# Two-layer recurrent block on one core: retention products and the last gather moved in the slot order, B taken ahead of the gate, and half of the rank comparisons replaced by row sums

## The reference

```
xn = layernorm(x)
s  = retention(xn)                      # q k^T with decay GAMMA^(i-j), times v
g  = silu(w3 . gelu(h2 . gelu(h1 . (silu(w1 xn) * (w2 xn)))))    # ternary weights, 512 hidden
x  = x + s * g
xn = layernorm(x)
a, gate = split(xn @ W_in + b_in)
xc = silu(causal_conv4(a))
B, C = split(xc @ W_x + b_x)            # 16 states
h_t = A * h_(t-1) + xc_t (x) B_t        # a scan over the sequence for 128 x 16 states
s  = ((C_t . h_t) + D * xc_t) * silu(gate) @ W_out + b_out
# mixture of depths: the 512 best of 1024 tokens by the router's score get an update
w  = sigmoid(top-512 scores);  g = silu(xn + [token chosen] * w * ffn(xn))
x  = x + s * g
```

## Time and profile before

| | us |
|---|---|
| median of three runs | 546.86 |
| lowest, highest | 544.11, 549.14 |
| the profiled execution | 545.56 |
| its span (first to last instruction) | 543.8 |

### The profile page before, as it was taken

One profiled execution on the slowest core, in us unless ns is written; L12 is line 12 of the kernel. 1 busy time (PEld: TensorE's weight loads), 2 busy tenths in 40 slices (PEclk: granted clock), 3 DMA queues, 4 the chain that ended last, 5 costly groups with the idle time before them and its releaser, 6 DMA issues.

```text
span 543.8 us, 6040 instructions
## 1 busy us (share of the span) xinstructions
PE 443.4 (82%) x1777; PEld 259.0 (48%) x1791; DVE 407.9 (75%) x659; ACT 291.4 (54%) x475; POOL 404.7 (74%) x316
## 2 busy tenths in 40 slices
PE   0796978898889897989899888989798999485743
PEld 0575645644564455545565456445554464131211
DVE  2282144959788977989598959898789779958985
ACT  3664736774567545763676366745676447313300
POOL 1673543887599959985999769985999599855582
PEclk9997979899999999999999999999999999978865
DMA  8300006311513143221532162214321332215220
GB/s 316 136 20 4 1 0 175 85 51 40 155 60 86 50 125 108 77 77 47 152 96 78 37 176 77 79 39 118 115 79 58 96 99 78 78 44 165 85 74 19
DMA packets 25379, 46.97 MB, mean 86 GB/s; under 512 B 3072, under 2 KB 4096, under 8 KB 25088
## 3 DMA queue, kind: packets, MB, share of 16 engines
q1 hardware_dynamic: 24336, 45.13, 28.1%
q10 hardware_dynamic: 1008, 1.41, 0.8%
HBM read 42.33 MB, written 4.19 MB: 86 GB/s over the span
## 4 chain that ended last, share of the span: by engine, by line
POOL 35%; DVE 23%; issue 17%; PE 16%; ACT 5%; DMA 1%; SPq 0%; DVEq 0%; POOLq 0%; ACTq 0%
POOL hs L548 15%; DVE hs L1359 10%; PE bank0a L932 7%; DVE xbank L1336 7%; POOL hidAl L510 6%; POOL hidBl L510 5%; PE bank1a L1012 2%; POOL xnTl L492 2%; POOL g L526 2%; POOL g L522 2%; DMA Bt<-w_in 1%; POOL xr L530 1%; POOL q L499 1%; PE ybank L1071 1%; DVE st L1262 1%
## 5 line engine op out<-in xcount | busy, mean ns | idle before, releaser
L548 POOL TENSOR_TENSOR hs<-hs,Ct 128x512 f32<-128x512 f32 x127 | 184.6, 1459 | 32.6 <-DVE hs L1359 19.7
L510 POOL TENSOR_TENSOR hidAl<-plain,hidAh 128x512 fp32r<-128x512 f32 x48 | 64.6, 1346 | 37.7 <-ACT hidAh L643 31.3
L1359 DVE TENSOR_TENSOR_SCAN hs<-decay,carry,xbank 128x512 f32<-128x512 f32 x63 | 80.5, 1278 | 7.6
L510 POOL TENSOR_TENSOR hidBl<-plain,hidBh 128x512 fp32r<-128x512 f32 x48 | 66.1, 1378 | 26.6 <-ACT hidBh L643 18.7
L1359 DVE TENSOR_TENSOR_SCAN hs<-decay,xbank 128x512 f32<-128x512 f32 x64 | 78.0, 1219 | 5.6 <-DVE xbank L1336 0.5
L1336 DVE TENSOR_TENSOR xbank<-xs,bbank 128x512 f32<-128x512 f32 x104 | 71.4, 687 | 1.3
L642 ACT ACTIVATE plain<-bank0a,col 128x512 f32<-128x512 f32 x64 | 44.2, 690 | 45.2 <-PE bank0a L932 44.0
L932 PE MATMUL bank0a<-hidBh,hTh 128*128 128x512 f32 x128 | 57.7, 451 | 1.7 <-ACT q L675 1.7
L932 PE MATMUL bank0a<-hidAh,hTh 128*128 128x512 f32 x128 | 57.0, 445 | 1.7 <-ACT q L675 1.7
L932 PE MATMUL bank0a<-hidAl,hTh 128*128 128x512 f32 x128 | 51.6, 403 | 0.0
L932 PE MATMUL bank0a<-hidBl,hTh 128*128 128x512 f32 x128 | 50.7, 396 | 0.0
(11 more groups left out here) (184 smaller groups left out, 951.7 us busy)
## 6 DMA issues: line engine op xcount, KB each, us to landing
xs<-x_rows SPq DMA_DIRECT2D x128, 256.0 KB, 3.4
xt<-x_tok SPq DMA_DIRECT2D x8, 256.0 KB, 4.5
xr<-x_feat SPq DMA_DIRECT2D x8, 256.0 KB, 7.6
x_rows<-xc SPq DMA_DIRECT2D x8, 256.0 KB, 2.0
out<-xr SPq DMA_DIRECT2D x7, 256.0 KB, 2.2
fh<-h_w SPq DMA_DIRECT2D x1, 1024.0 KB, 10.0
hs<-h_w SPq DMA_DIRECT2D x1, 1024.0 KB, 11.9
lw<-l_w ACTq DMA_DIRECT2D x1, 640.0 KB, 5.4
```

The lines of the kernel that those rows point to most:

```text
L510: pool.tensor_tensor(low[:, m, :], plain[:, k % NPLAIN, :], high[:, m, :].bitcast(F32), ALU.subtract).then_inc(hidden_low, 1)
L548: pool.tensor_tensor(h, h, Ct[:, hs_(u)], ALU.mult).then_inc(p_ready, 1)
L1359: dve.tensor_tensor_scan(hs[:, i % NSTATES, :], decay[:, gr:gr + 1].broadcast_to([P, HALF]), xbank[:], 0.0 if u % 2 == 0 else carry[:, k:k ...
```

## The change

There are six edits.

1. `scores` goes from slot 2 to slot 4 of PE, and `outer` from the end of slot 4's list to slot 5, behind B's projection and ahead of the gate's. `mask_scores` goes from slot 2 to 4 and `memory` from 4 to 6 on DVE, and `scale_q` from 5 to 6 on POOL. The order of `bank0d` becomes z2 of tile 1, z2 of tile 3, scores, outer.
2. The projection of B goes ahead of that of the gate, on PE and on ACT (`take_B` directly behind the conv).
3. `stats_l0` goes from slot 7 to 5 on DVE and `rstd_l0` from 8 to 6 on POOL.
4. `gather_y` of the last quad goes from slot 8 to 9, behind `retention_out` and `retention_in`; `gate_y` from 9 to 11. The last unit keeps its slot.
5. Odd units no longer do `compare_other`. The even unit before compares in four instructions of 512 columns whose row sums (`counts`) tell for each token of the odd unit how many tokens of the even one beat it. In the rank of the odd unit four small matmuls with the identity bring these counts in place of four matmuls over comparisons. In the even unit's rank the comparison is turned round, so it is summed with a matrix of minus ones and compared with TOPK - HALF.
6. The same order in the run-in: `scores(0)` behind all of z2, the mask behind all four `z_product`.

```diff
@@ orders of the banks
-        L0_DVE += [("z2", _v, 1), ("scores", _v), ("z2", _v, 3), ("outer", _v)]
+        L0_DVE += [("z2", _v, 1), ("z2", _v, 3), ("scores", _v), ("outer", _v)]
-        L1_ACT += [(_k, _n) for _k in ("xnT", "conv", "gate", "B", "C", "score", "score_col")]
+        L1_ACT += [(_k, _n) for _k in ("xnT", "conv", "B", "gate", "C", "score", "score_col")]
@@ POOL slot
-                if w is not None and s == 8:
+                if w is not None and s == 6:
                     rstd_l0(w)
                 if u is not None:
                     weigh_states(u, k)
-                if v is not None and s == 5:
+                if v is not None and s == 6:
                     scale_q(v)
@@ ACT slot
                     if s == 5:
                         convolved(n)
+                        take_B(n)
                         take_gate(n)
...
-                    if s == 6:
-                        take_B(n)
-                    elif s == 7:
+                    if s == 7:
                         take_C(n)
@@ PE rank
-                    pe.wait_ge(beats_ready, r + 1)
-                    pe.matmul(bank1d[:], ones[:], beats[:, r % NBEATS, :], start=(pos == 0),
-                              stop=(pos == CH - 1)).then_inc(l1_dve_full if pos == CH - 1 else ranked, 1)
+                    full = l1_dve_full if pos == CH - 1 else ranked
+                    if u % 2 == 1 and pos >= CPH:
+                        j = pos - CPH
+                        pe.matmul(bank1d[:, ck(j)], counts[:, j:j + 1].broadcast_to([P, P]), ident[:], start=False,
+                                  stop=(pos == CH - 1)).then_inc(full, 1)
+                        return
+                    pe.wait_ge(beats_ready, beats_of(u) + pos + 1)
+                    pe.matmul(bank1d[:], ones[:] if pos < CPH else minus_ones[:], beats[:, r % NBEATS, :],
+                              start=(pos == 0), stop=(pos == CH - 1)).then_inc(full, 1)
@@ PE slot
-                        elif s == 2:
+                        elif s == 4:
                             scores(v)
-                        elif s == 4:
-                            outer(v)
...
                         elif s == 5:
-                            project("gate", n, W_IN[:, P:2 * P])
-                        elif s == 6:
                             project_x("B", n, W_B)
+                    if v is not None and s == 5:
+                        outer(v)
+                    if n is not None and s == 5:
+                        project("gate", n, W_IN[:, P:2 * P])
...
-                    if s == 8 and t is not None:
-                        gather_y(t, 3)
...
+                    if t is not None and s == (8 if t == UNITS - 1 else 9):
+                        gather_y(t, 3)
@@ DVE compare_other
-                other = u // 2 * 2 + 1 - u % 2
...
-                dve.tensor_tensor(beats[:, CPH:], row.broadcast_to([P, CPH, HALF]), s_i.broadcast_to([P, CPH, HALF]),
-                                  ALU.is_le if u % 2 else ALU.is_lt).then_inc(beats_ready, CPH)
+                for j, c in enumerate(chunks(u + 1)):
+                    dve.tensor_scalar(beats[:, CPH + j, :], srow[:, hs_(u)], scol[:, u // 2 % 2, c:c + 1], 0.0, ALU.is_ge,
+                                      ALU.add, accum_out=counts[:, j:j + 1]).then_inc(beats_ready, 1)
@@ DVE slot
-                    if s == 2:
+                    if s == 4:
                         mask_scores(v)
-                    elif s == 4:
+                    elif s == 6:
                         memory(v)
                 if t is not None:
-                    if compare_slots(t)[CPH] == s:
+                    if t % 2 == 0 and compare_slots(t)[CPH] == s:
                         compare_other(t)
...
-                    elif t < UNITS - 1 and s == 9:
+                    elif t < UNITS - 1 and s == 11:
                         gate_y(t)
...
-                    if s == 7:
+                    if s == 5:
                         stats_l0(w)
```

More of the change, by code:

```diff
@@ L118, in compare_slots, with beats_of @@
     return (-5, -4, -3, -2) + ((0, 0, 0, 0) if u == UNITS - 1 else (10, 10, 10, 10))
+def beats_of(u):
+    return u // 2 * (CH + CPH) + u % 2 * CH
 def rank_slots(u):
@@ L207, in program @@
         ones = sb("ones", [P, P], BF16)
+        minus_ones = sb("minus_ones", [P, P], BF16)
+        counts = sb("counts", [P, CPH])
         half_neg = sb("half_neg", [P, CH])
@@ L470, in _ @@
             pool.memset(ones[:], 1.0).then_inc(consts_set, 1)
+            pool.memset(minus_ones[:], -1.0).then_inc(consts_set, 1)
             pool.memset(earlier[:, 0:HALF - P], 0.0).then_inc(earlier_ready, 1)
@@ L579, in slot @@
                     add_output(e)
-            pool.wait_ge(consts_set, 3)
+            pool.wait_ge(consts_set, 4)
             rstd_l0(0)
@@ L698, in take_scores @@
                 if t >= 2:
-                    act.wait_ge(beats_ready, (t - 1) * CH)
+                    act.wait_ge(beats_ready, beats_of(t - 1))
                 take1(("score", t), srow[:, hs_(t)])
@@ L1171, in rest @@
                             retention_q(0)
-                        elif m == 2:
-                            scores(0)
+                    scores(0)
                     outer(0)
@@ L1187, in _ @@
             rest(exact=False, first=True)
-            pe.wait_ge(consts_set, 3)
+            pe.wait_ge(consts_set, 4)
             pe.wait_ge(l1_params, 16 * NPARAM_L1)
@@ L1308, in compare_other @@
             def compare_other(u):
-                other = u // 2 * 2 + 1 - u % 2
-                dve.wait_ge(l1_act_done, done(L1_ACT, ("score_col", other)))
+                dve.wait_ge(l1_act_done, done(L1_ACT, ("score_col", u + 1)))
                 if u > 0:
                     full1(("rank", u - 1))
-                s_i = scol[:, u // 2 % 2, cs_(other)].rearrange("p (c o) -> p c o", o=1)
-                row = srow[:, hs_(u)].rearrange("p (o i) -> p o i", o=1)
-                dve.tensor_tensor(beats[:, CPH:], row.broadcast_to([P, CPH, HALF]), s_i.broadcast_to([P, CPH, HALF]),
-                                  ALU.is_le if u % 2 else ALU.is_lt).then_inc(beats_ready, CPH)
+                for j, c in enumerate(chunks(u + 1)):
+                    dve.tensor_scalar(beats[:, CPH + j, :], srow[:, hs_(u)], scol[:, u // 2 % 2, c:c + 1], 0.0, ALU.is_ge,
+                                      ALU.add, accum_out=counts[:, j:j + 1]).then_inc(beats_ready, 1)
             def token_weights(t):
@@ L1321, in token_weights @@
                 full1(("rank", t))
-                dve.scalar_tensor_tensor(g1[:, hs_(t)], bank1d[:], float(TOPK), g1[:, hs_(t)],
+                dve.scalar_tensor_tensor(g1[:, hs_(t)], bank1d[:], float(TOPK if t % 2 else TOPK - HALF), g1[:, hs_(t)],
                                          ALU.is_lt, ALU.mult).then_inc(l1_dve_done, 1)
@@ L1430, in slot @@
                 if w is not None:
-                    if s == 7:
+                    if s == 5:
                         stats_l0(w)
-            dve.wait_ge(consts_set, 3)
+            dve.wait_ge(consts_set, 4)
             stats_l0(0)
@@ L1461, in _ @@
             z_product(0, 2)
+            z_product(0, 3)
             mask_scores(0)
-            z_product(0, 3)
             memory(0)
```

## The result

The changed kernel takes 562.87 us (median of 4 runs, 557.46 to 564.74) against 545.65 for the kernel before in the same comparison: ratio 1.029 with a 95% interval of 1.020 to 1.038. It is slower, as the likeliest case said, but by 17 us (16 against the median of 546.86 that the forecast started from) in place of 7, and the time lies above the range (537 to 561).

The account below looks back on a forecast made before the run. The prediction took GpSimd without gaps in one half of each period, and TensorE's path in the other, as the bound. 6 x (1.7 - 0.8) + 1 + 1.9 - 1.5 = +6.8 us on 546.86 gave 553.5, range 537 to 561.

Parts of the forecast that it names:

- the likeliest case: Whole kernel: slower, at 553.5 us, its own range 549.5 to 557.5, chance 0.40.
- The other half: From h2's last low part to the next h1's first: B and outer delay h1 by 2.0, net +1.7 us per period.
- GpSimd's wait ahead of h1's low part: Sign to look for: GpSimd's wait before the first low part of h1 grows from 5.1 to about 7 us.
- the one on gains: Mask off VectorE's path and TensorE's 1.79 us wait gone ahead of z2: 0.7 us gained, 0.3 kept per period.
- The GpSimd half: From h1's first low part to h2's last, GpSimd without gaps: scale_q +1.25, comparison relief -2.05, sum -0.8 us per period.
- the comparison's relief: GpSimd no longer slowed by VectorE's wide comparison during two weigh_states: -2.05 us per period, for even units too.
- The last rival: Even units' row sums slow GpSimd as the wide comparison did, +2.05 us each for three: 559.5 us, chance 0.18.
- Run-in: Start of the kernel: scores and mask between the fourth product and outer, less what z2 gains: +1 us.
- Unit 0's GpSimd half: Unit 0, first low part of h1 to last of h2, holding the branch on the weights: 0 us.
- Run-out: End of the kernel, VectorE's path: one comparison of 2.27 us gone, 0.4 wait back, four instructions +0.4: -1.5 us.
- faster: Rival: B and outer are hidden because TensorE's chain doesn't end GpSimd's wait; 539 to 531, taken as 537 us, chance 0.20.
- no change: Rival: larger relief, as VectorE products that slow GpSimd fall into its wait, -0.45 to -0.9 per period; 547.5 us, chance 0.22.

Follow-up runs that it names:

- e3_fill: The changed kernel with 14 dummy matmuls a period in TensorE's three gaps: 549.46 us, ratio 1.0086.
- e4_ret_back: The changed kernel with scores, outer, mask, memory and scale_q back in their old places, run-in included: 545.01 us, ratio 1.0006.
- e7_gates_stats: The kernel before with row-sum counts, statistics sooner, and the last gather and gate_y later: 537.65 us, ratio 0.981.
- e2_order: The changed kernel with the wide comparison as before in place of the row-sum counts: 571.54 us, ratio 1.049.
- e1_counts: The kernel before with only the row sums and counts in place of the odd units' wide comparison: 538.13 us, ratio 0.9875.
- e6_runin_back: The changed kernel with the old order of scores and mask in the run-in alone: 558.46 us, ratio 1.021.
- e5: The kernel before with 14 dummy matmuls a period in TensorE's own three gaps, a control: 551.04 us, ratio 1.0079.
- e10: e3_fill without the four dummy matmuls ahead of the last gather: 550.42 us, ratio 1.0067.
- e11: e3_fill with scale_q back in GpSimd's slot 5, ahead of the first low part of h1: 544.62 us, ratio 0.9975.
- e8: e1_counts with 20 dummy matmuls ahead of the branch on the weights: 534.12 us, ratio 0.979.
- e9: e7_gates_stats with 20 dummy matmuls ahead of the branch on the weights: 531.41 us, ratio 0.971.
- e12: e9 with 11 more dummy matmuls in unit 0's second layer: 530.19 us, ratio 0.971.

## Why the prediction was wrong

**The other half, +1.7: right for what it priced, and the size was missed, +2.5 on the mean of six.** With the gaps filled (e3_fill) it is +1.9 and +1.6, and e4_ret_back and e7_gates_stats show B as its cause. GpSimd's wait ahead of h1's low part grew from 5.1 to between 8.7 and 10.5 us, not to 7; with the clock at 1.00 it is 8.7 to 9.0. By the forecast's own terms it had to be 8.0, since scale_q leaves the place ahead of the wait: 5.1 + 1.7 + 1.2. The step that failed is the one on gains: "TensorE no longer waits 1.79 us ahead of z2 of tile 3", scores take outer's place, "I take 0.3". It took the moved wait for idle time that costs what it lasts. It now stands next to the wait for yn, and behind the pair the clock can fall to half: 1.5 us in the half shown above. Over six halves the trace has 4.9 us more than forecast; e3_fill takes 4.0 of them back.

**The GpSimd half, -0.8: right in its parts, a little better as a sum.** Scale_q cost 1.05 (e2_order) against 1.25, the comparison's relief 1.75 (e7_gates_stats) against 2.05; the measured sum is -1.25. The two parts make -0.7; where the other 0.55 comes from was not taken apart. The relief was 1.75 a period with edits 3 and 4 beside it and 0.8 without (e1_counts), so these two were not at 0 either. The last rival, that row sums slow GpSimd, gives nearly the right time (559.5) for a wrong reason: GpSimd's operations beside them take 1.26 to 1.28 us, and its pair of weigh_states later on 2.53. The Trainium skill (VectorE: DVE Perf Modes, the perf-mode tier table) has fp32 tensor_scalar at 2x, but its row is for the plain instruction, and the forecast carried it over to the one with a row sum. That one took 0.74 us here for 512 columns, no faster than VectorE's other single passes of that width, such as the 0.75 us product in the earlier trace rows. So the rule of the Trainium skill on contention (GPSIMD Engine Reference, section Specifications) is not contradicted: the row sums read one SBUF tensor and show no sign of a faster mode.

**Run-in, +1: mis-sized, +4.5.** The order's cost was there (e6_runin_back takes 4.0 back), but scores wait 2.64 us behind the fourth product and then run at half clock: 2.08 us in place of 1.16, and outer 2.04 in place of 1.13. The changed kernel:

```profile
29.12 2.08 PE L904 MATMUL bank0d<-q,xnT 128*128 128x128 f32 x8 [2.64 <-DVE plain L1262]
32.07 2.04 PE L912 MATMUL bank0d<-xn,xt 128*128 128x128 f32 x8 [0.88 <-DVE sc L1238]
```

**Unit 0's GpSimd half, 0: wrong by 2.8, and for a reason that lies in no line of the change.** Behind the branch TensorE stops a second time. The busy time by stretch of the changed kernel shows nothing running at 53 to 54 us:

```profile
51.00:52.00 1.00, 0.48 (x2) 0.51 (x3) 0.00 (x0) 0.97 (x2) 0.00 (x0) 0.50 0.00 0
52.00:53.00 1.00, 0.29 (x2) 0.20 (x1) 0.00 (x0) 0.06 (x1) 0.00 (x0) 0.50 0.05 16
53.00:54.00 1.00, 0.00 (x0) 0.00 (x0) 0.00 (x0) 0.00 (x0) 0.00 (x0) 0.50 0.00 0
```

The one transfer there, at 52 to 53, is on the queue of instructions. In all five kernels that stop a second time such a transfer of 16 KB starts within 0.3 us of the stop's start. Kernels without the stop have one at about the same place too (at 47.55 us in the kernel before, where TensorE went on at 47.03), so the transfer alone doesn't decide it. Over all kernels this half takes 27.8 to 28.7 us with that second stop (the changed kernel, e1, e4, e6, e7), 24.7 to 25.2 without it (before, e2, e3, e5, e10, e11), and 23.0 to 23.6 with dummies ahead of the branch (e8, e9, e12). I read it as code that arrives late, depending on where in the program it falls; that was not tested by itself, and the cause of this term stays open. The Trainium skill (Runtime: NRT & Kernel Launch, section Instruction fetch mechanics) says that a taken branch can stall until its target has been fetched by DMA; the trace agrees, as far as it goes, by that transfer.

**Run-out, -1.5: mis-sized, -5.0.** Kernels with edit 5 but without edits 1 and 2 end 104.0 to 106.9 us after the last unit's first low part of h1 (e1, e7, e8, e9, e12), before 110.6, and the changed kernel 105.6; without edit 5 it is 111.7 (e2_order). So it is edit 5 that gains there, and more than was forecast. What of the run-out gave it was not taken apart.

**The rest, 5.4 us from the profiled execution to the median, stays open.** The changed kernel's runs spread over 7.3 us. The mean granted clock of each execution is on record: 0.928 for the fastest (557.46 us), 0.925 for 561.19, 0.920 for 564.54 and 0.923 for 564.74. So the clock is the first candidate, and the same gap cost 0 to over 2 us from one period to the next; but there is no trace of a slower execution.

**The rivals.** B and outer weren't hidden (faster), and the relief wasn't larger than the clock's loss (no change). The lower edge of the forecast's own range, 549.5 to 557.5, is where the kernel stands once its gaps are filled (549.5, 550.4), but not term by term. The trace of e3_fill has +3.1 us in place of +6.8: the GpSimd halves (-8.4) and the run-out (-3.2) came out better than forecast and the start (+2.8) worse. What was missing was a rival for the clock.

## What to carry to other kernels

When a move closes one wait of TensorE and opens another, look at where the idle times end up next to each other, not only at their sum: before, 1.79 and 0.79 us lay apart and cost their length; after, 1.74 and 1.23 us with 0.63 of work between them, and pairs like it, took up to half their speed from the matmuls behind them in four of six periods. If such a gap can't be closed, a few dummy matmuls in it are worth trying, and they only cost where the clock isn't falling. And price every edit by itself: here the counts gained 6.6 us on the whole, while B lost 2.0 us in each period and scale_q 1.05.

## What the runs showed of the hardware

- The same gaps cost differently from one period to the next: waits of 1.74 and 1.23 us took the granted clock to 0.50 in the period at 254 us and left it at 1.00 in the one at 373. Scores behind a wait of 1.23 us took 1.16 (twice), 1.23, 1.33, 1.48 or 2.08 us in the six middle periods of the changed kernel.
- A comparison with a row sum of 512 columns takes VectorE 0.74 us and an accumulator read of 0.08 behind it, 0.67 from start to start, and leaves GpSimd at 1.26 us; the wide comparison of two SBUF tensors that it replaces held a pair of GpSimd operations at 4.59 us, 2.53 without it.
- In the eleven kernels without matmuls ahead of the branch TensorE stood still there for 4.8 to 5.3 us, and in five of them for another 2.1 to 2.7 us two matmuls later. Twenty matmuls ahead of the branch did not shorten the first stop (5.2 in place of 5.4 us to the first matmul behind it), but behind them the clock was at 1.00 (products of 128 columns began 0.22 us apart in place of 0.43), and all three kernels that had them lacked the second one. Whether the matmuls took it away or the place of the code in the program, which they shift, the runs don't tell apart.
